# Graph attention on one core: the edges' logits move from VectorE's sums to TensorE's accumulation and products

## What is computed

```python
x_l, x_r = (x @ W_l).reshape(n, H, C), (x @ W_r).reshape(n, H, C)
e = (ea @ W_e).reshape(-1, H, C)                       # ea: 32 features of each edge
m = jax.nn.leaky_relu(x_l[src] + x_r[dst] + e, 0.2)
alpha = jnp.einsum('ehc,hc->eh', m, att)               # the logits
amax = jax.ops.segment_max(alpha, dst, num_segments=n)
expa = jnp.exp(alpha - amax[dst])
denom = jax.ops.segment_sum(expa, dst, num_segments=n)
out = jax.ops.segment_sum(x_l[src] * (expa / (denom[dst] + 1e-16))[:, :, None], dst, num_segments=n)
```

## Time and profile before

| | |
|---|---|
| median of 3 runs | 2248.37 us (2243.04 to 2249.6) |
| span of the profiled execution | 2249.7 us |
| TensorE, VectorE, ScalarE, GpSimd busy | 1665.0, 1504.7, 969.8, 916.3 us |
| first and last gather of attention start at | 984.64 and 2141.25 us |
| end of attention | about 2187.6 us |

### The profile page before, as it was taken

How to read it: one execution, slowest core, us unless ns; L and a number is a source line. 1 busy time by engine, 2 the same in 40 slices (tenths; PEclk the granted TensorE clock), 3 DMA queues, 4 the chain that set the end, 5 groups by cost and what they waited for, 6 DMA issues and landing times. The chain is left out here.

```text
span 2249.7 us, 34161 instructions
## 1 busy us (share of the span) xinstructions
PE 1665.0 (74%) x10041; PEld 1359.7 (60%) x10041; DVE 1504.7 (67%) x3141; ACT 969.8 (43%) x2263; POOL 916.3 (41%) x880
## 2 busy tenths in 40 slices
PE   5566666899799999865667677766777767776756
PEld 2455555655478887634566666666666656666744
DVE  4766666577744342477677777867777867787875
ACT  0355565677455234430234434434434335344535
POOL 1000000000100000037777777777777777777800
PEclk9555555799999999988788988888888898898877
DMA  2100000000034000034333333333343333333211
GB/s 70 60 1 1 1 1 1 8 0 0 29 87 130 27 1 6 14 100 96 92 90 91 97 93 91 92 96 92 87 100 94 86 95 97 91 93 93 60 39 29
DMA packets 134433, 136.86 MB, mean 61 GB/s; under 512 B 28689, under 2 KB 105074, under 8 KB 134258
## 3 DMA queue, kind: packets, MB, share of 16 engines
q0 software_dynamic: 27776, 60.71, 12.2%
q1 hardware_dynamic: 106482, 73.98, 11.5%
HBM read 129.67 MB, written 4.92 MB: 60 GB/s over the span
## 5 line engine op out<-in xcount | busy, mean ns | idle before, releaser
L2112 POOL DMA_INDIRECT rows<-x_l,src x856 | 896.9, 1048 | 292.5 <-issue 260.1
L2180 PE MATMUL psum<-both,node_hot 128*128 128x144 f32 x1712 | 304.1, 332 | 202.0 <-DVE both L2374 175.2
L2180 PEld LDWEIGHTS psum<-both,node_hot 128*128 128x128 f32 x1712 | 264.7, 222 | 229.4 <-issue 197.4
L2127 PE MATMUL psum<-w_e,edges 128*128 128x272 f32 x856 | 323.9, 466 | 56.7 <-DVE z L2287 46.9
L2129 PEld LDWEIGHTS psum<-x_r,hot 128*128 128x128 f32 x1712 | 313.8, 224 | 51.1
L2129 PE MATMUL psum<-x_r,hot 128*128 x1712 | 313.1, 312 | 0.0
L2287 DVE TENSOR_TENSOR z<-psum,rows 128x544 f32<-128x544 f32 x214 | 154.3, 721 | 235.4 <-issue 163.7
L2237 ACT ACTIVATE apart<-iota,minus_rel 128x128 f32<-128x128 f32 x828 | 261.9, 386 | 0.0
L769 ACT ACTIVATE counts<-psum (+1 forms) x181 | 181.5, 1003 | 175.8 <-PE psum L762 112.1
L1145 POOL TENSOR_TENSOR ht<-ht,mix_rows 128x512 f32<-128x512 f32 (+1 forms) x7 | 7.8, 1149 | 587.4 <-ACT mix_rows L1186 587.4
L1260 PE MATMUL psum<-halves,counts 128*128 128x257 f16 (+1 forms) x1725 | 198.1, 277 | 7.4 <-DVE halves L1465 3.9
(11 more groups left out here) (335 smaller groups left out, 2187.3 us busy)
## 6 DMA issues: line engine op xcount, KB each, us to landing
rel_row<-e_rel_rows SPq DMA_DIRECT2D x107, 256.0 KB
edges<-edge_t SPq DMA_DIRECT2D x428, 32.0 KB
rows<-x_l,src POOLq DMA_INDIRECT x856
edge_part<-edge_t SPq DMA_DIRECT2D x40, 320.0 KB, 3.1
x_r<-x_l SPq DMA_DIRECT2D x1, 1632.0 KB
ht<-x SPq DMA_DIRECT2D x6, 256.0 KB, 2.8
new<-e_new_before SPq DMA_DIRECT2D x12, 128.0 KB
new<-e_new_behind SPq DMA_DIRECT2D x12, 128.0 KB
```

Of the source, the lines that this page charges most:

```text
L2112: e.indirect_dma_start(rows[:, g % ring, j * ROW:(j + 1) * ROW], None, k.xl, bass.IndirectOffsetOnAxis(ap=src[:, at:at + 1], axis=0)).then ...
L2127: e.matmul(pair[:, j // 2, :], edges[:, r, :], w_e[:, j:j + 2, :].rearrange("p j f -> p (j f)"), start=True, stop=False)
L2180: final = e.matmul(to, near_hot[:, at, j, :], both[:, at, j, :], start=j % 2 == 0, stop=j % 2 == 1)
```

## The change

The rows lose the 17th column (128 columns in place of 136). For group g, with the channels now on the partitions and the edges along the free side:

- TensorE `begin(g)`, one slot ahead, accumulates into one of three banks of 512 columns: `x_r`'s rows, split into three bf16 parts whose sum they are, times `hot` (now bf16), 6 products of 256 columns; and `w_e` times the edges' features, one fp32 product of 512 columns over 32 partitions.
- TensorE `join(g)` adds the gathered rows, turned, by four products with the identity (128 columns each). GpSimd's gathers now wait for `joined`.
- ScalarE `slope(g)` writes 0.2 z to `bent`; VectorE `bend(g)` takes the maximum of z and that.
- TensorE `head_sums(g)` multiplies `bent` by `att_heads` (512 columns), shifted so that the group's 8 lines fall on their partitions; the products of a batch accumulate in one bank, in which the logits then lie as the scans want them. It comes two slots later, for the last group of a batch one slot later, and first in TensorE's slot. `turn_alpha` is gone.

The orders within a slot are now: TensorE `head_sums`, `begin(t+1)`, `join(t)`, the turns, `sum_rows`; ScalarE `keep_ends`, `keep_weights`, `fill`, `slope(t)`, `exponentials`; VectorE `one_hots(t+2)`, `weigh`, `add`, `bend(t)`, then the rest. The three parts of `x_r` are made by `RowParts.split`, 4 instructions for each 5 blocks: the first on GpSimd in `project`, the other four on VectorE in slots 0 to 3. `own_logits` moves to slots 5 to 9 and has 5 instructions in place of 4. The edges have 3 places in place of 6. `by_pair` lies in `rows`, of `firsts` only one value a batch is loaded, `apart` and `begins` are bf16.

```diff
+                def begin(g):
+                    two, z = g % 2, z_banks[g % 3]
+                    blocks = [block_of.at(2 * g + j) for j in range(2)]
+                    due_parts = min(2 * g + 1, s.nb - 1) // 5
+                    if due_parts > min(max(2 * g - 1, 0), s.nb - 1) // 5:
+                        e.wait_ge(split.sem, split.at(4 * due_parts))
                     e.wait_ge(hots.sem, hots.at(g + 1))
-                    e.wait_ge(edge_here[r].sem, edge_here[r].at(2 * lap(g)))
-                    if g >= 2:
-                        e.wait_ge(sums.sem, sums.at(g - 1))
+                    if g >= 3:
+                        e.wait_ge(leaky.sem, leaky.at(g - 2))
+                    for j in range(2):
+                        half = slice(j * 2 * P, (j + 1) * 2 * P)
+                        for q in range(3):
+                            e.matmul(z[:, half], row_parts.parts[:, bass.ds(blocks[j], 1), q, :].rearrange("p o f -> p (o f)"),
+                                     hot[:, two, half], start=j + q == 0, stop=False)
+                    e.wait_ge(edge_here[g % edge_slots].sem, edge_here[g % edge_slots].at(edge_lap(g)))
+                    e.matmul(z, w_e[:, :], edges[:, g % edge_slots, :], start=False, stop=False).then_inc(*products.up())
+
+                def join(g):
+                    z = z_banks[g % 3]
+                    e.wait_ge(got[g % slots].sem, got[g % slots].at(4 * lap(g)))
                     for j in range(4):
...
+                        final = e.matmul(z[:, j * P:(j + 1) * P], rows_at(g)[:, j * P:(j + 1) * P], k.ident[:, :],
+                                         start=False, stop=j == 3)
+                    final.then_inc(*joined.up())
+
+                def head_sums(g):
+                    b = batch_of(g)
+                    c = g - b.first
+                    low = LINES - HEADS - c * HEADS
+                    e.wait_ge(leaky.sem, leaky.at(g + 1))
+                    if c == 0 and b.i >= 2:
+                        e.wait_ge(weights.sem, weights.at(2 * (b.i - 1)))
+                    e.matmul(alphas_of(b), k.att_heads[:, low:low + b.lines], bent[:, g % 3, :],
+                             start=c == 0, stop=c == b.n - 1).then_inc(*alphas.up())
...
-                logits(0)
+                begin(0)
                 for t in range(len(due)):
+                    for g in summed_in(t):
+                        head_sums(g)
                     if t + 1 < groups:
-                        logits(t + 1)
-                    for piece, turn in ((0, turn_alpha), (1, turn_ends), (2, turn_carries), (5, turn_weights)):
+                        begin(t + 1)
+                    if t < groups:
+                        join(t)
+                    for piece, turn in ((1, turn_ends), (2, turn_carries), (5, turn_weights)):
...
+                def slope(g):
+                    e.wait_ge(joined.sem, joined.at(g + 1))
+                    if g >= 3:
+                        e.wait_ge(alphas.sem, alphas.at(g - 2))
+                    e.activation(bent[:, g % 3, :], z_banks[g % 3], ACT.Copy, scale=NEG_SLOPE).then_inc(*sloped.up())
...
-                def add_rows(g):
...
                 def bend(g):
-                    heads = z[:, g % 2, :].rearrange("p (v h c) -> p v h c", v=4, h=HEADS)[:, :, :, 0:CH]
-                    e.wait_ge(sums.sem, sums.at(g + 1))
-                    e.scalar_tensor_tensor(heads, heads, 0.0, att_of(k, 4), ALU.max, ALU.mult).then_inc(*leaky.up())
+                    e.wait_ge(sloped.sem, sloped.at(g + 1))
+                    e.tensor_tensor(bent[:, g % 3, :], z_banks[g % 3], bent[:, g % 3, :], ALU.max).then_inc(*leaky.up())
```

```diff
+    def split(self, e, c, done):
...
+        e.tensor_copy(part[0], self.xr[:, at, :]).then_inc(*done.up())
...
+        e.tensor_tensor(rest[:, :, :], self.xr[:, at, :], part[0], ALU.subtract).then_inc(*done.up())
...
+        e.tensor_copy(part[1], rest[:, :, :]).then_inc(*done.up())
...
+        e.tensor_tensor(part[2], rest[:, :, :], part[1], ALU.subtract).then_inc(*done.up())
```

More of the change, by code:

```diff
@@ L19 @@
 CH = D // HEADS
-ROW = HEADS * (CH + 1)
+ROW = D
+LINES = 16 * HEADS
 DE = 32
@@ L1795, in project @@
         projected, kept, kept_r = k.flag("projected"), k.flag("x_l_kept"), k.flag("x_r_kept")
-        flat = [w[:, j, :, :].rearrange("p h c -> p (h c)") for j in range(3)]
-        both = w[:, 0:2, :, :].rearrange("p j h c -> p (j h c)")
+        split = k.flag("x_r_split")
+        both = raw[:, 0:2, :].rearrange("p j f -> p (j f)")
         with k.nc.Block() as block:
@@ L1965, in schedule, with attention @@
     return slots
-def attention(k, x, h, xr, w_e, acc, rows, own, loops, tables):
+def attention(k, x, h, xr, w_e, acc, rows, own, loops, tables, row_parts):
     s, io, groups = k.s, k.io, k.s.groups
     steps = 2 * s.padded
-    ring, slots, ahead, deep, lag = RING, 6, 4, 4, 22
+    ring, slots, edge_slots, deep, lag = RING, 6, 3, 4, 22
     wide = D + 2 * HEADS
@@ L2043, in attention, with summed_in, edge_lap, bank_of @@
         totals, added = k.flag("totals"), k.flag("added")
-        turn_bank, misc = k.bank[4], k.bank[5]
+        split = k.flag("x_r_split")
+        z_banks, misc = (k.bank[0], k.bank[1], k.bank[4]), k.bank[5]
+        def summed_in(t):
+            ends = [b.over - 1 for b in plan]
+            return [g for g in (t - 2, t - 1) if 0 <= g < groups and (g == t - 1) == (g in ends)]
         def lap(g):
             return 16 * (g // slots + 1)
-        def pair_of(g):
-            return k.psum[:, 2 * (g % 2):2 * (g % 2) + 2, 0:2 * ROW]
+        def edge_lap(g):
+            return 2 * 16 * (g // edge_slots + 1)
+        def bank_of(b):
+            return k.bank[2 + b.two]
+        def alphas_of(b):
+            return bank_of(b)[0:b.lines, :]
         def by_head(j, b):
@@ L2117, in _ @@
             def _(e):
-                def logits(g):
-                    r, two, pair = g % slots, g % 2, pair_of(g)
-                    node_rows = [xr[:, bass.ds(block_of.at(2 * g + j), 1), :].rearrange("p o f -> p (o f)") for j in range(2)]
-                    e.wait_ge(hots.sem, hots.at(g + 1))
-                    e.wait_ge(edge_here[r].sem, edge_here[r].at(2 * lap(g)))
-                    if g >= 2:
-                        e.wait_ge(sums.sem, sums.at(g - 1))
-                    for j in range(4):
-                        if j % 2 == 0:
-                            e.matmul(pair[:, j // 2, :], edges[:, r, :], w_e[:, j:j + 2, :].rearrange("p j f -> p (j f)"),
-                                     start=True, stop=False)
-                        final = e.matmul(pair[:, j // 2, j % 2 * ROW:(j % 2 + 1) * ROW], hot[:, two, j * P:(j + 1) * P],
-                                         node_rows[j // 2], start=False, stop=j % 2 == 1)
-                    final.then_inc(*products.up())
@@ L2253, in _ @@
                         fill(u)
+                    if t < groups:
+                        slope(t)
                     b = batch_at(t, 4)
@@ L2427, in _ @@
                         weigh(u)
-                    if t < groups:
-                        bend(t)
                     for u in due[t - 1] if t else []:
```

190 lines of the change are left out of this document (99 added, 91 removed).

## The result

The kernel after takes 2253.64 us (median of 20 runs, 2249.47 to 2258.15); beside it the kernel before took 2245.21 us (20 runs, 2240.33 to 2254.27). The ratio is 1.0034, its 95% interval 1.0026 to 1.0042: slower by 8 us, where 28 us faster than the median shown then was forecast.

The account below looks back on a forecast made before the run. GpSimd's gathers were taken to bound the kernel. 2249.7 - 31.0 (less gather stretch) + 2 (start and end) = 2220.7 us; with the runs' median 1.3 us below the span, 2220 us, range 2190 to 2268.

Parts of the forecast that it names:

- The gathers bound the kernel before: GpSimd sets the pace from 984.6 to 2141.2 us, at 1.25 us for each of 856 gathers.
- The change takes 31.0 us from the gathers: GpSimd: less stretch from `bend` -32.7, shorter one-hot -1.8, more blocking work at the start +3.5; sum -31.0 us.
- rival 2: Gathers lock onto VectorE's `weigh`, caught in over a third of the slots: 39 us more, 2260; in all, 2310; chance 0.13.
- Rival 3: Gathers lock clear of VectorE's `weigh`, the lower bound: 54 us off, 2196 us; chance 0.15.
- rival 4: The gathers' stretch comes from any work, not from `bend`: they keep 86 us, 2250 us; chance 0.06.
- TensorE's slot is 4.3 us: TensorE's work for a group rises from 2.8 to 4.3 us, against gathers of 5.0 plus about 0.2.
- the cover holds, thinly: TensorE's batch of 16 takes 79 us with one clock fall, against the gathers' 83, so it stays hidden.
- rival 1: TensorE becomes the bound: 86 us a batch gives 2250, 90 gives 2300; likeliest 2250 (2240 to 2275); chance 0.22.
- The stall of `turn_carries`, 3.5 us each, stays: TensorE: `turn_carries` waits for `scan_ends`, 49.5 us in 14 times, 3.5 each; that stays.
- `slope` behind the fill costs 1 to 1.5 us for each piece: ScalarE's late `slope` makes `bend` 3 to 4 us late; TensorE waits 1 to 1.5 us for `both`.
- In slots with two sums TensorE falls behind: +3.5; with the shorter last chain +2: End: TensorE needs 5.3 us in two-sum slots, +3.5 us; the chain behind the last group -1.5; together +2.
- A late batch evens out before GpSimd stops: Rows can be fetched 6 groups ahead of `join`, five slots of slack, so GpSimd isn't stopped by a late batch.

Follow-up runs that it names:

- e3: Kernel before with the fourth gather of each group left out from group 28 on; 2060.68 us, ratio 0.9182 to the kernel before.
- e6: Kernel before with `turn_carries` one slot later in TensorE's list; 2245.59 us, ratio 1.0015 to the kernel before.
- e1: Kernel after with two of the three bf16 parts of `x_r` left out of TensorE's products; 2250.19 us, ratio 1.0012 to the kernel before.
- e4: Kernel after with `turn_carries` one slot later in TensorE's list; 2225.16 us, ratio 0.9905 to the kernel before.
- e7: Kernel after with `slope` ahead of `keep_ends`, `keep_weights` and `fill` in ScalarE's list; 2221.96 us, ratio 0.9913 to the kernel before.
- e17: Kernel after with the fourth gather left out from group 28 on and two of three bf16 parts of `x_r` left out; 2198.48 us, 0.9795.
- e5: Kernel after with TensorE's waits for edges and gathered rows moved ahead of `begin`'s products; 2256.58 us, ratio 1.0041 to the kernel before.
- e16: Kernel after with `slope` first and `turn_carries` one slot later, in the second slow-chip set; 2386.78 us.
- e11: Apparently (by order) kernel after with `slope` first, `turn_carries` later, and an extra maximum with both inputs in SBUF, in the first slow-chip set; 2415.45 us.
- e8: Kernel after with `slope` first on ScalarE and `turn_carries` one slot later; 2208.48 us, ratio 0.9837 to the kernel before.
- e10: Kernel after with `slope` first, `turn_carries` later, and the fourth gather left out from group 28 on; 2186.95 us on a slow chip.

## Why the prediction was wrong, by its steps

- *The gathers bound the kernel before.* Right, shown by `e3` (0.9182) and `e6` (1.0015).
- *The change takes 31.0 us from the gathers.* Right: 31.6 us, first start to last. Put down as before, no gather ends 0.82 us behind the maximum, and `weigh` (now L2426) holds 80 gathers and 37.6 us, where 16.3 + 20.2 = 36.5 was worked out. That is over a third of the slots, which rival 2 had as its condition, but at 0.47 us each and in the sum already, so its 39 us more didn't come. Rival 3 neither; rival 4 is refuted by this and by the pair with the extra maximum. The Trainium skill ("SBUF — State Buffer", Who interferes with whom) says that a VectorE instruction with two SBUF inputs contends with a GpSimd instruction that reads SBUF, and the pair agrees (43 and 52 gathers against none). The prediction called the section's inferred remark on writing descriptors contradicted; that goes too far. Each gather also reads its 128 source numbers, `src`, from SBUF, and no run here tells that reading from the writing of descriptors.
- *TensorE's slot is 4.3 us.* Mis-sized: 4.64. `begin` took 0.75 (0.71), the edges 1.05 (0.87), `join` 1.00 (0.87), the sum 0.98, the head sums 0.86. The product over 32 partitions and what follows it were priced by columns alone. The 0.34 us more are 5.4 us a batch, more than the margin of 4. The batch from 1573.08 to 1656.94 took 83.9 us, where 79 was taken and the gathers need 83. So "the cover holds, thinly" failed by what was called thin; rival 1, with 86 a batch, has the place and nearly the time (2250). That is in part luck: it counted on falls of the clock in every batch, where the granted clock was 0.96, and it put nothing on the last 37 groups, which lose 28.5 us. Nor is TensorE the cause alone, as `e1` shows: work taken from it gives nothing while the gathers keep 5.2 us.
- *The stall of `turn_carries`, 3.5 us each, stays.* The size held or was below (39.6 us in 14, 2.8 each), its price didn't: with a thin margin every stop is on the path, and the half clock behind it too. Priced by `e4`: 29 us.
- *`slope` behind the fill costs 1 to 1.5 us for each piece.* Too much for the middle: TensorE's waits for `both` are 7.3 us in 17, none over 0.7, and `e7` saves only 2.0 us up to group 176. Too little for the last batches: a single wait for `bent` was 5.03 us, and `e7` saves 28.1 us there.
- *In slots with two sums TensorE falls behind: +3.5; with the shorter last chain +2.* **This is the step that failed.** The last 37 groups cost 28.5 us more. The sum had only their work in it (5.3 us a slot, measured 5.62). It left out that the batches of 10, 6 and 6 bring a batch's stops every 10 and then every 6 slots, that `keep_weights` and two fills stand ahead of a `slope` whose head sums close the next batch, and that each stop is followed by work at about half clock (0.50 to 0.65 over the 2.7 us behind each `turn_carries`). `e17` shows that less work alone doesn't cure it; `e7` and `e4`, which leave the work and turn the order, take back 28.1 and 19.8 us of it.
- *A late batch evens out before GpSimd stops.* True for GpSimd (15.5 us of waits) and beside the point: the gathers were done at 2107.8, and the last `slope` came 45 us later, where before 4 us lay between them.

The two edits don't add up: by their ratios against 1.0034, `e4` saves 29 us, `e7` 27, both together 44. What part of the end is owed to each stop was not measured.

## What to carry to other kernels

When work moves onto an engine that had slack, price its list by its stops: every wait that the slack had hidden, and the slower clock behind it, now counts. Taking work away may not help while the stops stay. Look for the stretch of the schedule where the stops come closest together (here the short batches with two sums a slot), and work that one out slot by slot. Put the instruction that another engine is waiting for ahead of those with a slot to spare; here two small moves in the lists turned a loss of 0.3% into a gain of 1.6%.

## What the hardware showed beyond that

- A product's columns don't tell all of its time. In the slot above the edges' two records of 512 columns, over 32 partitions, took 1.05 us to the next product (1621.47 to 1622.52), the head sums' two of the same size over 128 partitions 0.86 (1624.50 to 1625.36). In the trace the load of the weights behind the edges starts at 1622.52, together with its product; the one behind the head sums starts at 1624.93, 0.43 us ahead of it. Moving the waits (`e5`) changed nothing. Why the first isn't made ahead isn't shown.
- In the sets in which before took 2514 to 2519 us, `slope` started late behind the recorded end of its `join`: a median of 1.74 us in `e16` (150 copies from 1080 to 1980 us) and 1.03 in `e11`, against 0.04 in `e8`, the same kernel as `e16`. Here `join` ends at 1312.97 and `slope` starts 2.44 us later, though ScalarE had been idle for 4.20:

```profile
1311.81 1.16 PE L2183 MATMUL psum<-ident,rows 128*128 128x128 f32 x8
...
1315.41 0.60 ACT L2280 ACTIVATE bent<-psum 128x512 f32<-128x512 f32 x1 [4.20 <-DMA w<-L_gnn_W_self_t]
```

  With three gathers a group (`e10`, in the set of `e11`) it was 0.04. What delays it stays open.
